# Handing every 56th gather of two edge sums from GpSimd to SyncE, row by row

## The reference

```python
def _L0_gnn_ref(x, A_indices, A_values, A_shape, W, bias, gamma, beta):
    h = jnp.einsum('nd,df->nf', x, W)
    gathered = A_values[:, None] * h[col]
    agg = jax.ops.segment_sum(gathered, row, num_segments=A_shape)
    ...                                   # + bias, normalise over nodes, relu
def _L1_gnn_ref(feat_in, edge_row, edge_col, edge_val, W1, b1, W2, b2, eps, offset, scale):
    msg = edge_val[:, None] * feat_in[edge_col]
    aggr = jax.ops.segment_sum(msg, edge_row, num_segments=feat_in.shape[0])
    aggr = aggr + (1.0 + eps) * feat_in
    h = jnp.maximum(aggr @ W1 + b1, 0.0) @ W2 + b2
    ...                                   # relu, normalise each row
x = x + _L0_gnn_ref(_layernorm(x, axis=-1), edge_index, edge_weight, ...)
x = x + _L0_ffn_ref(...)                  # feed-forward on the better half of the nodes
x = x + _L1_gnn_ref(_layernorm(x, axis=-1), src, dst, edge_weight, ...)
x = x + _L1_ffn_ref(_layernorm(x, axis=-1), ...)   # 8 experts, two per node
```

## Time and profile before

| | |
|---|---|
| time, median of 3 runs | 3943.59 us (3941.09 to 3946.39) |
| span of the profiled execution | 3521.7 us |
| median less span: what lies around the span | 421.9 us |
| first edge sum, first to last gather | 385.2 to 1369.7 us |
| second edge sum, first to last gather | 1786.1 to 2771.4 us |
| POOL gathers (L1081) | 784 in each sum, 952 ns each |
| PE products of the slots (L1174) | 1087.2 us busy in both sums |

### The profile page before, as it was taken

How to read it: one execution, slowest core, us unless ns; L and a number is a source line. 1 busy time by engine, 2 the same in 40 slices (tenths; PEclk the granted TensorE clock), 3 DMA queues, 4 the chain that set the end, 5 groups by cost and what they waited for, 6 DMA issues and landing times. The chain is left out here.

```text
span 3521.7 us, 55765 instructions
## 1 busy us (share of the span) xinstructions
PE 2647.4 (75%) x15311; PEld 2239.6 (64%) x15311; DVE 2613.3 (74%) x6603; ACT 1008.4 (29%) x2073; POOL 2208.3 (63%) x2147
## 2 busy tenths in 40 slices
PE   6888466666666665899967677777776569999998
PEld 4777344454444444789945555555555459999997
DVE  6999566666666666969967777777777778888886
ACT  0011000000000002545511111111111168888886
POOL 0455577777777774345557777777777326666664
PEclk9999687878878787899978888888788779999999
DMA  3011433333333332000133333333333447776775
GB/s 98 10 44 33 120 105 105 105 105 105 105 105 105 105 105 73 1 2 31 37 103 111 113 112 111 113 113 111 113 111 113 133 134 216 213 218 211 219 211 140
DMA packets 164679, 389.01 MB, mean 110 GB/s; under 512 B 46378, under 2 KB 95602, under 8 KB 151019
## 3 DMA queue, kind: packets, MB, share of 16 engines
q0 software_dynamic: 99072, 233.49, 24.4%
q1 hardware_dynamic: 65387, 152.94, 12.8%
HBM read 343.97 MB, written 42.98 MB: 110 GB/s over the span
## 5 line engine op out<-in xcount | busy, mean ns | idle before, releaser
L1081 POOL DMA_INDIRECT g_got<-table,e_source x1568 | 1492.1, 952 | 506.5 <-issue 458.9
L1174 PE MATMUL psum<-g_got,g_route 128*128 x3328 | 1087.2, 485 | 642.0 <-DMA g_got<-table,e_source 253.6
L1174 PEld LDWEIGHTS psum<-g_got,g_route 128*128 128x128 f32 x3328 | 760.9, 239 | 888.4 <-issue 763.5
L1107 DVE TENSOR_TENSOR A<-A,psum 128x256 f32 x1664 | 698.5, 420 | 523.6 <-PE psum L1174 345.1
L1090 DVE TENSOR_SCALAR g_route<-columns,e_local,e_weight 128x128 f32<-128x128 f32 x1664 | 472.5, 363 | 17.7 <-issue 12.9
L368 POOL DMA_INDIRECT records<-rec,place x120 | 148.7, 1239 | 220.6 <-ACT rec L580 122.0
L1582 POOL TENSOR_TENSOR f_ht_lo<-f_ht,f_ht_hi 128x512 fp32r<-128x512 f32 x100 | 133.7, 1341 | 187.8 <-ACT f_ht_hi L1531 182.1
L142 PE MATMUL psum<-e_xt_hi,e_w_hi 128*128 128x256 f32 x832 | 238.0, 286 | 5.5 <-issue 5.3
L142 PE MATMUL psum<-e_w_hi,e_ht_hi 128*128 128x256 f32 x832 | 233.1, 280 | 3.1 <-DVE e_w_lo L1981 3.1
L144 PE MATMUL psum<-e_xt_hi,e_w_lo 128*128 128x256 f32 x832 | 233.8, 281 | 0.0
L143 PE MATMUL psum<-e_xt_lo,e_w_hi 128*128 128x256 f32 x832 | 233.7, 281 | 0.0
(11 more groups left out here) (420 smaller groups left out, 5198.5 us busy)
## 6 DMA issues: line engine op xcount, KB each, us to landing
e_w<-in_m_w SPq DMA_DIRECT2D x104, 1024.0 KB, 5.0
g_got<-table,e_source POOLq DMA_INDIRECT x1568, 2.8
expert_table<-g_normal SPq DMA_DIRECT2D x52, 128.0 KB
table<-xn SPq DMA_DIRECT2D x49, 128.0 KB, 1.7
X<-in_x SPq DMA_DIRECT2D x1, 6144.0 KB
table<-f_ring SPq DMA_DIRECT2D x24, 256.0 KB, 2.1
out<-X SPq DMA_DIRECT2D x1, 6144.0 KB
f_w<-in_f_w SPq DMA_DIRECT2D x2, 1024.0 KB, 7.3
```

Source lines behind the costliest of these rows:

```text
L1081: pool.indirect_dma_start(got[:, c % RING, :], None, rows, bass.IndirectOffsetOnAxis(ap=source[:, c:c + 1].bitcast(U32), axis=0)).then_inc ...
L1107: dve.tensor_tensor(to, to, sums_of(c), ALU.add).then_inc(added, 1)
L1174: ins = pe.matmul(sums_of(c), route[:, c % (GB + GSEM), :], row(got, at[j % GSEM]), start=True, stop=True)
```

## The change

Chunks 56k + 55 (k from 1) are no longer gathered by POOL but by SP, with one DMA for each of their 128 rows: 13 chunks (k = 1 to 13) in the first sum, and 12 (k = 1 to 13 without 6) in the second. These chunks have three places of their own (55, 56 and 57 of now 58, `place_of`), which they use in turn, each with a semaphore `hand_landed`. SP fetches the 128 row numbers of such a chunk in two halves from device memory into the buffer `expert` (`ask`), reads eight of them into registers with one `TENSOR_LOAD`, and then issues eight DMAs of one row; ahead of each stands a register operation for the row's address. In the first sum SP does so from its last parameter load on without a pause except for places and numbers. In the second it issues 112 rows first and then 32 rows after each `store_normal`. `slot_ring` is computed for the new places (six more small DVE instructions in `order_slots`). The buffer `normal` has two halves with a semaphore each; SP no longer waits for a store to land before it goes on, and `normalise` waits for the store of two tiles before.

```diff
+HAND = RING - 1
+HAND_PLACES = 3
+PLACES = HAND + HAND_PLACES
+ROUND = HAND_PLACES * RING
...
+def place_of(c):
+
+    return HAND + c // RING % HAND_PLACES if c % RING == HAND else c % RING
...
-                wait(dve, self.stored, k)
-                wait(dve, self.normal_turned, k)
-                dve.tensor_scalar(self.normal[:], row(X, t), self.ln_moments[:, 0:1], self.ln_inverse[:, 0:1],
+                wait(dve, self.stored[k % 2], 16 * (k // 2))
+                wait(dve, self.normal_turned, k - 1)
+                dve.tensor_scalar(self.normal[:, k % 2, :], row(X, t), self.ln_moments[:, 0:1], self.ln_inverse[:, 0:1],
...
-                             self.normal[:].rearrange("p (a d) -> p a d", a=1)).then_inc(self.landed, 16)
-                sp.wait_ge(self.landed, 16 * k + 16)
-                sp.sem_inc(self.stored, 1)
+                             self.normal[:, k % 2:k % 2 + 1, :]).then_inc(self.stored[k % 2], 16)
...
+            def ask(self, sp, i, h):
+                c = self.chunks[i]
+                sp.dma_start(self.numbers[:, h, :], kept_fields[0][h * self.HALF:(h + 1) * self.HALF, c:c + 1].rearrange("p a -> a p"),
+                             allow_slow_non_contiguous=True).then_inc(hand_numbers_in, 16)
+
+            def fetch(self, sp, got, rows, pairs_summed, start, end):
+
+                for r in range(start, min(end, P * len(self.chunks)), self.LOAD):
+                    i, p = divmod(r, P)
+                    h, c = p // self.HALF, self.chunks[i]
+                    if r == 0:
+                        self.ask(sp, 0, 0)
+                    if p == 0 and c >= ROUND:
+                        sp.wait_ge(pairs_summed, (c - ROUND + NT - 1) // 2 + 1)
+                    if p % self.HALF == 0:
+                        sp.wait_ge(hand_numbers_in, 16 * (2 * (self.before + i) + h + 1))
+                    _, nodes = nc.values_load_multi_w_load_instructions(
+                        self.numbers[0:1, h, p % self.HALF:p % self.HALF + self.LOAD], engines=(mybir.EngineType.SP,), min_val=0, max_val=NT * P - 1,
+                        skip_runtime_bounds_check_because="a source is a node")
+                    for j in range(self.LOAD):
+                        sp.dma_start(got[p + j:p + j + 1, place_of(c), :], rows[bass.ds(nodes[j], 1), :]).then_inc(hand_landed[(self.before + i) % HAND_PLACES], 16)
+                    if p % self.HALF == 0 and i + h < len(self.chunks):
+                        self.ask(sp, i + h, 1 - h)
...
+        turns = [range(1, CHUNKS // RING), [t for t in range(1, CHUNKS // RING) if t != 6]]
...
+                    HANDED_FIRST, HANDED = P - 2 * hand.LOAD, 4 * hand.LOAD
...
+                        hand.fetch(sp, got, rows, pairs_summed, 0, P * CHUNKS)
                         sp.wait_ge(params, 144)
                     if through_mlp:
+                        handed = lambda k: HANDED_FIRST + k * HANDED
+                        hand.fetch(sp, got, rows, pairs_summed, 0, handed(0))
                         for k in range(FINISHES):
                             tiles_of.store_normal(sp, k, tile_to_finish(k + 1, mybir.EngineType.SP))
+                            hand.fetch(sp, got, rows, pairs_summed, handed(k), handed(k + 1))
                         tiles_of.store_normal(sp, FINISHES, last_tile(sp))
+                        tiles_of.wait_stored(sp)
...
                             for c in range(first, first + GSEM // 2):
+                                if c in hand.chunks:
+                                    continue
...
                             for q in range(asked[0], landed_by(first) + 1):
                                 pe.wait_ge(gathered[q % 8], gathered_after(q))
+                                hand.wait_landed(pe, q)
```

More of the change, by code:

```diff
@@ L840, in __init__ @@
                 self.wr = here("wr", [P, KD, NE])
-                self.normal, self.normal_t = here("normal", [P, D]), here("normal_t", [P, D])
+                self.normal, self.normal_t = here("normal", [P, 2, D]), here("normal_t", [P, D])
                 self.ln_stat, self.ln_moments = here("ln_stat", [P, 6]), here("ln_moments", [P, 2])
@@ L845, in __init__ @@
                 self.ln_step = sem("g1_ln_step")
-                self.normal_ready, self.landed, self.stored = sem("g1_normal"), sem("g1_normal_landed"), sem("g1_normal_stored")
+                self.normal_ready, self.stored = sem("g1_normal"), [sem("g1_normal_stored0"), sem("g1_normal_stored1")]
                 self.normal_turned, self.normal_out = sem("g1_normal_turned"), sem("g1_normal_out")
@@ L960, in store_normal, with wait_stored @@
                 sp.dma_start(expert_table[:, 0:D].rearrange("(t p) d -> p t d", p=P)[:, bass.ds(t, 1), :],
-                             self.normal[:].rearrange("p (a d) -> p a d", a=1)).then_inc(self.landed, 16)
-                sp.wait_ge(self.landed, 16 * k + 16)
-                sp.sem_inc(self.stored, 1)
+                             self.normal[:, k % 2:k % 2 + 1, :]).then_inc(self.stored[k % 2], 16)
+            def wait_stored(self, sp):
+                for u in range(2):
+                    sp.wait_ge(self.stored[u], 16 * ((STEPS + 1 - u) // 2))
             def turn_normal(self, pe, k):
@@ L1001, in build, with __init__, wait_landed @@
         gathered = [sem(f"gathered{u}") for u in range(8)]
+        class HandRows:
+            LOAD = 8
+            HALF = P // 2
+            def __init__(self, turns, before):
+                self.chunks = [RING * k + HAND for k in turns]
+                self.before = before
+                self.numbers = expert[:].rearrange("a (h p) -> a h p", h=2)
+            def ask(self, sp, i, h):
[19 more added lines that the diff above has]
+                        self.ask(sp, i + h, 1 - h)
+            def wait_landed(self, pe, q):
+                for i, c in enumerate(self.chunks):
+                    if c // GSEM == q:
+                        pe.wait_ge(hand_landed[(self.before + i) % HAND_PLACES], 16 * P * ((self.before + i) // HAND_PLACES + 1))
@@ L1003, in aggregate, with gathers_of @@
+        hand_numbers_in, hand_landed = sem("hand_numbers_in"), [sem(f"hand_landed{u}") for u in range(HAND_PLACES)]
+        turns = [range(1, CHUNKS // RING), [t for t in range(1, CHUNKS // RING) if t != 6]]
+        hands = (HandRows(turns[0], 0), HandRows(turns[1], len(turns[0])))
+        def gathers_of(q, hand):
+            return [c for c in range(q * GSEM, (q + 1) * GSEM) if c not in hand.chunks]
         def aggregate(rows, name, through_mlp, source, local, weight):
@@ L1027, in gathered_after @@
                 def gathered_after(q):
-                    earlier = -(-(CHUNKS // GSEM - q % 8) // 8) if through_mlp else 0
-                    return (earlier + q // 8 + 1) * (16 * GSEM)
+                    own = sum(len(gathers_of(at, hand)) for at in range(q % 8, q + 1, 8))
+                    before = sum(len(gathers_of(at, hands[0])) for at in range(q % 8, CHUNKS // GSEM, 8)) if through_mlp else 0
+                    return 16 * (before + own)
                 def sums_of(c):
@@ L1165, in _ @@
                                 pe.wait_ge(gathered[q % 8], gathered_after(q))
+                                hand.wait_landed(pe, q)
                             asked[0] = landed_by(first) + 1
                             _, at = nc.values_load_multi_w_load_instructions(
-                                slot_ring[0:1, first:first + GSEM], engines=(mybir.EngineType.PE,), min_val=0, max_val=RING - 1,
+                                slot_ring[0:1, first:first + GSEM], engines=(mybir.EngineType.PE,), min_val=0, max_val=PLACES - 1,
                                 skip_runtime_bounds_check_because="the ring's places are below its size")
```

31 lines of the change are left out of this document (19 added, 12 removed).

## The result

Measured: 4621.39 us (median of 4 runs, 4613.22 to 4623.93) against 3944.99 us before (4 runs), ratio 1.1699 with a 95% interval of 1.1677 to 1.1721. The forecast was 3913 us, 3906 to 3970.

What follows compares the result with a forecast made beforehand. POOL's gather issue was taken to bound both edge sums; 13 and 12 gathers less save 16.3 + 15.1 = 31.4 us, and 3943.6 - 31.4 + 0.5 (slot map path) = 3912.7, forecast 3913 us, range 3906 to 3970.

Steps and rivals of the forecast that it cites:

- SP's price of a row: SP's one-row DMAs in both sums: 0.254 us plus an issue of 0.30, 0.554 us a row.
- the prediction's own limit: First sum: SP's rows must take at most 0.568 us each, an issue of 0.315, to end by POOL's new end.
- span and surroundings, is taken equal to the median, so the difference carries over: Whole kernel: the profiled execution is taken equal to the median time, so 31.4 us saved comes off 3943.6.
- the load of eight numbers: SP, after every eighth row: 0.269 + 7 x 0.009 + 0.0425 = 0.37 us with passage, 0.047 a row.
- POOL bounds both sums: Both edge sums run at POOL's pace; 13 and 12 gathers less gain 16.3 and 15.1 us.
- The second sum's lag room: Second sum: SP's stores may lag 35 us before `normalise` waits; forecast lag 12 us, at most 21.
- `order_slots` and the double buffer: Six more instructions, some 1.3 us, hidden up to perhaps 0.5; second half of `normal` frees nobody on the path.
- PE's new waits: PE's 25 waits for handed chunks in the two sums cost nothing when the rows are there.
- SP becomes the bound: Rival at SP's row issue, both sums: decides from about 0.325 us an issue, 3960 to about 4270 us; chance 0.19.
- Two of its signs: Signs of wrong: issue above 0.32 us, PE waiting on line 1255 for SP's DMA, or DVE waiting at `normalise`.
- POOL itself slows: Rival in both sums: POOL's gathers take 0.06 us more beside SP's issues, 93 us, so 4005 us; chance 0.06.
- The rule against the change: SP's row issue: 512 sequencer cycles, estimated 0.427 us; the first sum would end some 172 us later than now.

Runs made afterwards that it cites:

- second trace of before: The unchanged kernel before, run again for a trace beside the first experiments: 3937.65 us (0.9997), span 3936.2 us.
- block version: Changed kernel, but SP brings each of the 25 handed chunks as one DMA of 128 consecutive table rows: 3920.19 us (0.9976); repeats 0.9983 and 0.9975.
- that run: Changed kernel without handing over: POOL gathers all 784 chunks of both sums, buffers and place table stay; 3939.86 us (0.9996).
- increments: Changed kernel without handing over, each SP row replaced by three semaphore raises that nobody reads: 4112.39 us (1.0464).

## Why the prediction was wrong

- **The step that failed** is SP's price of a row, 0.254 us plus an issue of 0.30, which the prediction carries through both sums whatever POOL does. On the chips that gave the times a row took 0.974 us on the mean of the first sum and 1.64 to 1.7 us beside POOL's gathers; the prediction's own limit was 0.568. What the sum lacks is a term of 1.1 us (1.64 less 0.54) for SP being held up while POOL gathers. It cost 447 us in the first sum through PE's waits and 193 in the second through the late stores.
- **Why the term was missed** is the sentence that joined trace and times: the profiled execution's time, "span and surroundings, is taken equal to the median, so the difference carries over". The trace (span 3521.7, clock 0.868) matches a chip of the 3520 kind, the times 3940 chips. The 421.9 us were no launch; 365 us of them are longer sums (from POOL's first gather to its last 1157.6 and 1175.1 us against 983.3 and 984.1). No row holds the second term: in the earlier trace rows SP issued beside POOL without harm, while in the second trace of before the same loads go from 0.43 to 0.70 us after the fourth.
- **On the 3520 chip** the price of 0.554 us was near: 0.534 measured, last row at 1303.5 where 1330 was forecast. That is in part luck. The issue was 0.225 us, below the whole range of 0.29 to 0.43, so an address in a register does not lengthen it; but the load of eight numbers, priced at 0.33 us, took 0.78. The one error takes 0.075 us off a row, the other puts 0.056 on. The prediction also misread its trace where it says that all but one of SP's issues took 0.33 or more: 46 of them took 0.32, three 0.29, and a one-row store (L335) 0.25.
- **POOL bounds both sums**: right on the 3520 chip, where the gain was 24.9 us of 31.4 (the interval, 17 to 34 us, holds the forecast) and the sums alone gained 30. On the 3940 chips POOL stops once in 16 chunks for the late signals, so that the mean pitch is 1.48 and 1.50 us; there 25 gathers less shortened the sums by 37 and 45 us (block version). This step did not fail.
- **The second sum's lag room** of 35 us held on the 3520 chip, where `normalise` waited for no store, and fell on the 3940 chips: DVE waited 37 times for a store. The mechanism (rows ahead of stores) was named, its size wrong by the same second term.
- **`order_slots` and the double buffer**: nothing measurable, as forecast (0.9996). PE's new waits were not in that run; on the 3520 chip nobody waited at them.
- **The rival** "SP becomes the bound" had the right place and consequence. Its price was sought in the issue, at 0.33 to 0.43; it came from POOL's gathers. 0.974 a row goes beyond all its cases, of which the dearest has 0.684. Its chance of 0.19 went by the trace of a chip that does not show it. Two of its signs came true (PE's wait on line 1255, DVE's at `normalise`), a median issue above 0.32 did not. "POOL itself slows" was wrong on both kinds: 952 and 953 ns a gather.
- **The rule against the change.** The Trainium skill, "DMA: Bandwidth & Descriptors", section "Why a DMA increments its semaphore by 16 and not by 1", states 512 cycles for a DMA instruction, 0.427 us by the estimate in the prediction. This does not hold for a one-row DMA with a computed address on either kind of chip: 0.225 us where nothing holds SP up. It named the right side for another reason.

Not settled: what in POOL's gather holds up the other engines' instructions and signals, and why only on some chips. Shown is that it is gone when POOL brings consecutive rows with ordinary DMAs (scattered rows without the gather instruction were not tried), that SP's DMAs are not needed (increments suffer too), that a limit on gathers under way and a busier gap don't cure it, and that it ends when POOL pauses. The block version was not measured on a 3520 chip. Of the 6 us that the changed kernel lacks there, the trace says that they lie outside the sums, but it was taken in an execution of 3500.45 us, where the other two took 3494.6 and 3494.8.

## What to carry to other kernels

Compare a profile's span with the times of the same kernel before any sum: where they differ by more than a few us, find out which stretch holds the difference, and treat "another chip, another bound" as a rival with a chance. Beside a stream of gathers by list on POOL, don't count on a long stream of small instructions on another queue; 13 large DMAs a sum cost nothing that shows on the 3940 chips. Where a test kernel moves other data than the real one, compare stages and not times: here the block version hid 37 us of gain behind two more rounds of a later stage. A change that relieves one chip by 0.7% can cost another 17%, so it is run on both before it is kept.

## What the hardware showed

- The same program takes 3520 us on two chips and 3931 to 3945 us on the others, each within 0.5% of its chip's median. Of the 415 us between the traces of before, 365 lie in the two sums, where POOL gathers by list.
- There an instruction of SP that takes 29 to 37 ns alone often takes 0.70 us beside POOL's gathers (one in eight, at most 1.4 us), and PE's count reaches DVE and POOL 9 to 13 us late, about 3 us after POOL's last gather.
- A one-row DMA (1 KB) with its address in a register takes 0.225 us of SP's time, a whole row 0.52 to 0.54 us with its share of the loads, undisturbed.
- On POOL, 0.12 us of other work after a gather is free on the 3520 kind; 0.32 us lengthens the mean pitch from 1.256 to 1.275 us.
